# Second attention: twelve full blocks of routed rows computed between its last steps

## What is computed

```python
# second attention, per batch of 256 tokens: x = layernorm(x + attention(x) @ Wo + bo)
# routed mixture: each token goes to its two best experts of eight
gates = softmax over the two largest of (x @ gate_w)
y_k   = gelu(x @ w1[expert_k] + b1) @ w2[expert_k] + b2     # 128 -> 512 -> 128
out   = layernorm(x + sum_k gate_k * y_k)
```

## Time and profile before

| | us |
|---|---|
| median of 3 runs | 1133.45 |
| lowest, highest | 1131.58, 1145.08 |
| the profiled execution | 1141.3 |
| its span | 1139.5 |
| PE, DVE, ACT, POOL busy | 969.8, 879.5, 737.4, 407.2 |
| mean granted TensorE clock | 0.924 of 2.4 GHz |

### The profile page before, as it was taken

One profiled execution on the slowest core, in us unless ns is written; L12 is line 12 of the kernel. 1 busy time (PEld: TensorE's weight loads), 2 busy tenths in 40 slices (PEclk: granted clock), 3 DMA queues, 4 the chain that ended last, 5 costly groups with the idle time before them and its releaser, 6 DMA issues. The chain is left out here.

```text
span 1139.5 us, 28905 instructions
## 1 busy us (share of the span) xinstructions
PE 969.8 (85%) x10214; PEld 617.3 (54%) x10214; DVE 879.5 (77%) x2343; ACT 737.4 (65%) x1411; POOL 407.2 (36%) x572
## 2 busy tenths in 40 slices
PE   4999999967789999999999994888887628888894
PEld 2788878743444444444444442565665417777731
DVE  5988999836889998688999984798888546677714
ACT  2666666638788888888888871555555216667614
POOL 3544454433433000000000002246777663555523
PEclk9999999968999999999999997899899559999967
DMA  8233322000012000322222211011111012222153
GB/s 264 101 106 121 120 101 71 4 2 19 1 57 85 1 1 1 98 74 74 74 75 80 77 47 31 29 29 39 42 47 39 30 57 67 69 66 65 49 142 93
DMA packets 60219, 72.59 MB, mean 64 GB/s; under 512 B 8858, under 2 KB 36764, under 8 KB 60080
## 3 DMA queue, kind: packets, MB, share of 16 engines
q1 hardware_dynamic: 51312, 60.05, 17.0%
q0 software_dynamic: 4544, 8.60, 2.3%
q10 hardware_dynamic: 4224, 2.10, 0.7%
HBM read 40.14 MB, written 31.49 MB: 63 GB/s over the span
## 5 line engine op out<-in xcount | busy, mean ns | idle before, releaser
L796 ACT ACTIVATE d__hf<-d__HB,dense__d 128x512 f32<-128x512 f32 x288 | 185.0, 680 | 39.7 <-PE d__HB L1022 38.7
L855 DVE TENSOR_TENSOR d__hl<-d__hf,d__hh 128x1024 f16<-128x1024 f32 x144 | 174.8, 1224 | 19.9 <-ACT d__hh L801 17.9
L801 ACT ACTIVATE d__hh<-d__hf 128x1024 f16<-128x1024 f32 x144 | 152.2, 1057 | 4.6
L769 POOL TENSOR_SCALAR d__rstd<-d__mv 128x4 f32<-128x4 f32 x16 | 14.7, 917 | 359.8 <-DVE d__mv L979 359.8
L1020 PE MATMUL d__YB<-d__hh,d__w2h 128*128 128x512 f16 x288 | 110.2, 383 | 3.0 <-DVE d__tmp L912 3.0
L1243 POOL DMA_INDIRECT parts<-c__ys,c__dest x78 | 83.3, 1068 | 79.1 <-ACT c__ys L1270 40.1
L1020 PE MATMUL d__HB<-d__xh,d__w1h 128*128 128x512 f16 x288 | 110.6, 384 | 0.0
L1021 PE MATMUL d__HB<-d__xl,d__w1h 128*128 128x512 f16 x288 | 110.5, 384 | 0.0
L1021 PE MATMUL d__YB<-d__hl,d__w2h 128*128 128x512 f16 x288 | 110.4, 383 | 0.0
L1022 PE MATMUL d__HB<-d__xh,d__w1l 128*128 128x512 f16 x288 | 110.2, 383 | 0.0
L1022 PE MATMUL d__YB<-d__hh,d__w2l 128*128 128x512 f16 x288 | 110.1, 382 | 0.0
(11 more groups left out here) (381 smaller groups left out, 2573.8 us busy)
## 6 DMA issues: line engine op xcount, KB each, us to landing
rows<-a__blank SPq DMA_DIRECT2D x72, 268.0 KB, 3.2
d__G<-gates SPq DMA_DIRECT2D x64, 256.0 KB, 3.1
c__xin<-rows SPq DMA_DIRECT2D x39, 134.0 KB
dense__stage<-e_w SPq DMA_DIRECT2D x16, 256.0 KB, 3.1
b__stage<-e_w SPq DMA_DIRECT2D x32, 128.0 KB, 2.3
c__yb<-parts SPq DMA_DIRECT2D x8, 256.0 KB, 8.4
c__yb<-parts ACTq DMA_DIRECT2D x8, 256.0 KB, 8.9
out<-c__xo SPq DMA_DIRECT2D x8, 256.0 KB, 2.3
```

The source lines that it names most:

```text
L796: act.activation(hf[:, q, f], HB[:, f], gelu, scale=1.0 / WS, bias=b1[:, at:at + 1]).then_inc(s_["h_free"], 1)
L801: act.activation(hh[:, j % (LEAD + 1), f - 1:f + 1], hf[:, q, f - 1:f + 1], ACT.Copy).then_inc(s_["hi_done"], 1)
L855: dve.tensor_tensor(hl[:, p, f], hf[:, q, f], hh[:, p, f], ALU.subtract).then_inc(s_["lo%d_done" % i], 1)
```

## The change

A new name, `routed`, is called after all other parts of each step from 16 on, on PE, ACT and DVE. A first table is computed in step 16 on DVE, from `base` as ten batches (five pairs) left it. It counts full blocks only (the 1 - BLOCK added to `many`) and names EARLY = 12 of them; `taken` keeps how many of each expert. These twelve blocks are computed after steps 18 to 21: three, four, three and two of them. They use one bank for the transposes (BC) and one for the sums (BD), where the loop of before alternates between two. SP loads their rows as soon as the first table and the sends of the first five pairs are done, and POOL scatters their results only after its last send, which is why RING (buffers of `ys`, `gate` and `dest`) goes from 6 to 12. The second table leaves out the blocks taken and names the other 27; it stands where the only table stood. The work of a block is the same, and there are 39 in all as before.

```diff
-RING = 6
+RING = 12
+EARLY, KNOWN = 12, 5
+AT_STEP = {18: range(0, 3), 19: range(3, 7), 20: range(7, 10), 21: range(10, EARLY)}
...
+        if s >= 16:
+            step("routed", s)
...
+    def turned_to(b):
+        bank = BC if b < EARLY else (BA, BB)[b % 2]
...
+    def summed_in(b):
+        bank = BD if b < EARLY else (BC, BD)[b % 2]
...
     def sync(sp):
-        sp.wait_ge(s["table_done"], 1)
         for b in range(NBLK):
+            if b in (0, EARLY):
+                sp.wait_ge(s["table_done"], 1 if b == 0 else 2)
...
-            if b == 0:
+            if b in (0, EARLY):
+                pairs = KNOWN if b == 0 else NB // 2
                 for p in range(SENT):
-                    sp.wait_ge(att["sent%d" % p], NB // 2 // SENT * 128)
+                    sp.wait_ge(att["sent%d" % p], (pairs - p + SENT - 1) // SENT * 128)
...
+    def scalar_early(act, step):
+        start, unit = scalar_units(act)
+        if step == 18:
+            start(0)
+        for b in AT_STEP.get(step, ()):
+            unit(b)
...
+    def table(dve, k):
...
+        if k == 0:
+            c.link(dve.tensor_scalar(many[:], many[:], 1.0 - BLOCK, None, ALU.add))
...
+        if k:
+            c.link(dve.tensor_tensor(nblk[:], nblk[:], taken[:], ALU.subtract))
...
+    def vector_early(dve, step):
+        start, unit = vector_units(dve)
+        if step == 16:
+            dve.wait_ge(s["loaded"], 16 * len(loads))
+            table(dve, 0)
+        if step == 18:
+            start(0)
+        for b in AT_STEP.get(step, ()):
+            unit(b)
...
     def vector(dve):
+        start, unit = vector_units(dve)
...
+        table(dve, 1)
+        start(1)
+        for b in range(EARLY, NBLK):
+            unit(b)
...
         def turned(b):
...
-            wait(pe, s["xt_done"], b - 1)
+            wait(pe, s["xt_done"], b if b < EARLY else b - 1)
...
         def down(b):
...
-            wait(pe, s["ys_done"], b - 1)
+            wait(pe, s["ys_done"], b if b < EARLY else b - 1)
...
+    def tensor_early(pe, step):
+        biases, start, unit = tensor_units(pe)
+        if step == 18:
...
+            biases(0)
+            start(0)
+        for b in AT_STEP.get(step, ()):
+            unit(b)
```

More of the change, by code:

```diff
@@ L1418, in down, with biases, start, unit @@
             ins.then_inc(s["y_full"], 1)
+        def biases(k):
+            b0, end = SPANS[k]
+            pe.wait_ge(s["table_done"], k + 1)
+            for f in range(FB):
+                ins = pe.matmul(BIAS[:, f, 0:end - b0], b1[:, f], mine[0:E, b0:end], start=True, stop=True)
+            ins.then_inc(s["bias_full"], 1)
+        def start(k):
+            for b in range(SPANS[k][0], SPANS[k][0] + 3):
+                turned(b)
+            pe.wait_ge(s["bias_done"], k + 1)
+            hidden(SPANS[k][0])
+        def unit(b):
+            end = EARLY if b < EARLY else NBLK
+            if b + 1 < end:
+                hidden(b + 1)
+            if b + 3 < end:
+                turned(b + 3)
+            down(b)
+        return biases, start, unit
+    def tensor_early(pe, step):
+        biases, start, unit = tensor_units(pe)
+        if step == 18:
+            pe.wait_ge(s["loaded"], 16 * len(loads))
+            pe.wait_ge(att["split_high"], NB)
+            pe.wait_ge(att["split_low"], NB)
+            pe.wait_ge(att["ctx_done"], NB)
+            pe.wait_ge(att["qt_done"], NB)
+            pe.wait_ge(att["keys_done"], 2 * NB)
+            pe.wait_ge(att["ots_done"], NB)
+            pe.wait_ge(att["lin_done"], NB)
+            biases(0)
+            start(0)
+        for b in AT_STEP.get(step, ()):
+            unit(b)
+    def tensor(pe):
+        biases, start, unit = tensor_units(pe)
         pe.wait_ge(s["act_out"], 1)
+        pe.wait_ge(s["xt_done"], EARLY)
         pe.wait_ge(att["gk_done"], NB // 2)
@@ L1425, in tensor @@
         pe.wait_ge(s["dve_out"], 1)
-        pe.wait_ge(s["loaded"], 16 * len(loads))
-        pe.wait_ge(s["table_done"], 1)
-        for f in range(FB):
-            ins = pe.matmul(BIAS[:, f], b1[:, f], mine[0:E], start=True, stop=True)
-        ins.then_inc(s["bias_full"], 1)
-        for b in range(3):
-            turned(b)
-        pe.wait_ge(s["gt_done"], 1)
-        pe.wait_ge(s["bias_done"], 1)
-        hidden(0)
-        for b in range(NBLK):
-            if b + 1 < NBLK:
-                hidden(b + 1)
-            if b + 3 < NBLK:
-                turned(b + 3)
-            down(b)
-        pe.wait_ge(s["loaded"], 16 * len(loads))
+        pe.wait_ge(s["ys_done"], EARLY)
+        biases(1)
+        pe.wait_ge(s["gt_done"], 1)
+        start(1)
+        for b in range(EARLY, NBLK):
+            unit(b)
         for q in range(NG):
@@ L1559, in attention_1 @@
         keep["ident16"] = ident16
-        early, sync, gpsimd, scalar, vector, tensor = blocks_1(nc, Mem(nc, ctx, "c"), d, keep, rows, parts, out,
-                                                               (SS, BA, BB, BC, BD), s)
+        (early, sync, gpsimd, scalar, vector, tensor, scalar_early, vector_early,
+         tensor_early) = blocks_1(nc, Mem(nc, ctx, "c"), d, keep, rows, parts, out, (SS, BA, BB, BC, BD), s)
         scale = float(HD) ** -0.5
```

134 lines of the change are left out of this document (86 added, 48 removed).

## The result

| | before | after |
|---|---|---|
| median, us | 1134.47 | 1162.83 |
| lowest, highest | 1131.58, 1145.08 | 1159.63, 1165.91 |
| the profiled execution, its span | 1141.3, 1139.5 | 1159.6, 1157.9 |
| mean granted clock | 0.924 | 0.931 |

The changed kernel is slower: ratio 1.0241, 95% interval 1.0206 to 1.0277. The forecast was no change, 1135.5 us in a range of 1119 to 1153.

The account below looks back on a forecast made before the run. Chain latency and POOL's sends set the loop's start; in the loop PE, DVE and ACT are near their limits together. First load +48.7, twelve blocks -45.4, table load -1.3: +2.0 us, median 1135.5, range 1119 to 1153.

Parts of the forecast that it names:

- The three things that set the loop's start: Ahead of the block loop: chain latency and POOL's late sends set its start, and the table does not.
- the one-bank pace: Early blocks: with one sum bank, `down` to the next takes 1.33 + 1.9 + 0.6 = 3.9 us, not 3.78.
- First table: DVE between step 16 and the maxima of step 17: nothing covers the table, +5.3 us, bounds 3.5 and 5.5.
- Steps 18 to 21: Attention's last steps with the early blocks: first row load moves from 935.1 to 983.8, +48.7 us, first table included.
- drains: ACT's table loads in step 20: a drain of about 1.4 us per switch could add up to 3 us.
- Twelve blocks leave: Block loop: twelve blocks fewer at 3.78 us each, -45.4 us.
- The loop fills again as before: Loop start: the same fill without ACT's table load between first `hidden` and first Gelu, -1.3 us.
- Nothing waits for POOL: Scatters queued behind POOL's last send end between 1083 and 1091, ahead of the last sum, with 3 us margin.
- B: Rival: early blocks stay at half clock, 6.2 us a block and not 3.9, +22 to +25 us, 1157 us; chance 0.14.
- A: Rival: the engines interleave better in the attention steps and early blocks, 12 us less, 1123.5 us; chance 0.20.
- C: Rival: POOL becomes the bound, scatters at 3.0 us a block end at 1099, final fetch 5 us late, 1140 us; chance 0.05.
- D: Rival: blocks fill all idle time of steps 18 to 21 and only the sends stay, 1105 us; chance 0.05.

Follow-up runs that it names:

- g2_after_gap: The changed kernel with a 128x512 memset on POOL behind every scatter, early and late, on a slower chip: 1161.54 us, ratio 1.0156.
- k2_after_block: The changed kernel with a 128x512 memset on POOL behind each block's second scatter, on a quicker chip: 1130.23 us, ratio 1.0250.
- e3_again: The kernel before with RING = 12 and 24 added indirect DMAs on POOL behind its last sends, on a slower chip: 1160.27 us, ratio 1.0200.

## Why the prediction was wrong

- **Read of before.** The three things that set the loop's start were right. The pace was misread: I put 3.78 us beside 2.9 us of PE's issue and called the rest waits between engines. Much of it is this effect: in the earlier trace rows the sum of block 26 waits 2.00 us for "remote", and POOL's train of four scatters ends at 1048.01, 0.65 us before ACT goes on. PE's updates for these sums come 1.3 to 1.9 us late in every second block; on the quicker chips, where they are not late, the loops take 3.02 to 3.09 us, so about 0.7 of the 0.9 us is gone. The trace of before held the clue, and I read the row for its start only. The 1.9 us of hand-over in the one-bank pace was the same late update.
- **First table.** PE's wait for the maxima grew from 1.63 to 7.79 us, as said (near 7). The matmul behind it came only 3.2 us later than before, but this execution was 3.0 us ahead when the table began. On DVE the table stands between 877.55 and the maxima at 883.71: 6.2 us, none of it covered, where 5.3 were priced.

```profile
885.59 0.53 PE L2058 MATMUL b__SS<-b__q,b__ks 32*128 32x128 f16 x12 [7.79 <-DVE b__mx L1876]
```

- **Steps 18 to 21.** The first load came 3.5 us under the forecast, and 3.0 of these are that start. First `hidden` 909.16 (forecast 910.7); the sums of blocks 2, 6 and 9 taken at 923.2, 945.8 and 962.3 (PE forecast to end at 925, 948, 966); `slots` done at 966.7 (971.6); last send issued at 976.6; first load at **980.28** (983.8). Taken from the same start, the sum of these steps was right to 0.5 us, with the table underpriced by 0.9 and the rest over by 1.4. Blocks 10 and 11 and the second table (969.40 to 975.33, 5.9 us) were hidden as said. Two table loads of 1.28 us stood in step 20, at 948.63 and 950.69, and no drain of 1.4 us shows: the 0.78 us between them hold three operations, and the Gelu starts 0.01 us after the second load. So the up to 3 us that the prediction set beside its sum for drains do not show.
- **Twelve blocks leave.** 46.5, forecast 45.4. Right on this chip, worth 36.5 on the quicker kind.
- **"The loop fills again as before" and "Nothing waits for POOL": the step that failed.** The term was -1.3 and measured +25.2. The loop did not fill as before, because POOL's train stood in front of it. I had asked whether POOL would be in time with its results, and whether its DMAs would be short of bandwidth or ring. I had not asked what a train of 24 does to engines that have nothing to do with it. In before no more than four scatters stand together in the loop, and the twelve sends lay where PE had hardly an update to give; the change put 8 + 24 behind each other with one pause of 0.9 us between, and the 24 lie in the one stretch in which PE, ACT and SP hand over at every step.
- **Rivals.** B (1157) came near in time and was refuted in mechanism: the early blocks ran at full clock but for their starts (granted clock 0.72 and 0.89 in the first two windows, 0.54 before), and the 0.59 of the refill is its idleness, as `g2_after_gap` shows by having none of the loss. A's gains did not show. C was priced at 5 us and 0.05; it did not bound the kernel as changed on the slower chips, but did so once gaps were put in (`g2_after_gap`, `k2_after_block`). D did not occur.
- **With the stall off**, 1162.8 - 25.2 = 1137.6: the sum of the other terms was good to 2 us. Part of that is luck, since the errors cancel: -0.5 for the first load (from the same start), -1.1 for the blocks that leave, +1.8 behind them. The range, 1119 to 1153, had no term for an engine's side effect on others, and so missed. Its lower bound was loosely built too: the terms named for it add up to -4.8, not -7.

## What to carry to other kernels

When work is postponed on a queue and then issued in one go, price the burst by what runs beside it, not only by whether its own results are late. Waits that the profile puts down to "remote" or "issue" and that end just when another engine pauses are a sign that the two are coupled, even with no dependency between them; the cheap test is to add a burst that nobody needs to the old kernel. Long runs of indirect DMAs can be loosened with gaps of 0.7 us or more, or spread, but both cost the issuing engine time: with a gap behind every scatter POOL became the bound, and no kernel with the early blocks was faster than before. Time the result on more than one chip. And compare two traces from a point ahead of the change, since one execution can be 3 us ahead of another there.

## What was unexpected in the hardware

- On the slower chips a run of indirect DMAs issued by POOL, 0.97 us each with 0.30 us between, made PE's semaphore updates late, some until 2.5 to 5 us after its end (ACT waited 28.6 us for one), and slowed most of SP's instructions to 0.70 us each; gaps of 0.71 us ended it, gaps of 0.39 us didn't; 24 plain DMAs did nothing of the kind. On the quicker chip where they were run, the same 24 had no such effect. That may be most of the 3% between the kinds: 39 blocks at 3.78 in place of 3.05 us are 28 us.
- Not settled: by what path the updates are held back; why some updates get through at once within a train (the biases of the kernel before, PE's end 928.10 and ACT's start 928.13, in the middle of twelve sends; the first two `turned` of `e3_again`); and whether the two kinds of chip differ in this alone.
- The kernel before ran its last f32 matmuls at half clock in the profiled execution and the changed one at full clock (pitch 2.00 against 1.06 us for a matmul of 512 columns), 7.4 us apart. None of the 18 traces of the experiments shows the half clock there: it is this one execution, and about the 7 to 8 us by which it lay above the median of before. Of before, then of after:

```profile
1101.98 2.08 PE L1453 MATMUL b__SS<-keep__xa,keep__ident 128*128 128x512 f32 x2
1103.98 2.07 PE L1451 MATMUL b__SS<-c__b,c__gts 32*128 32x512 f32 x2
```

```profile
1122.75 1.13 PE L1562 MATMUL b__SS<-keep__xa,keep__ident 128*128 128x512 f32 x2
1123.81 1.12 PE L1560 MATMUL b__SS<-c__b,c__gts 32*128 32x512 f32 x2
```
